# A four-layer graph kernel: VectorE takes the count tile of the next unit ahead of this unit's side items in the third layer, and one early maximum pass goes beside each unit

## Chip, cores and metric

One Trainium2 chip, one core of it. The metric is the time of one execution on the device in microseconds (us), as the median of several runs. A profile of one execution is read beside it.

## What is computed

A node table x of 3125 rows by 256 features goes through four layers, each of the form x = x + layer(max(layernorm(x), 0)), over one graph of 50000 edges (src, dst, weight):

```
L0: h + sum of neighbours -> (W1, batch norm, relu) -> (W2, batch norm, relu)
L1: two weighted graph convolutions with a root row, leaky relu, a linear layer
L2: x = norm * (h @ W.T + b);  out = norm * segment_sum(x[src], dst)
L3: a 4-head graph attention, graph norm, relu, a 1-head graph attention
```

`norm` is the degree to the power -1/2. The maximum in L3's softmax is taken over all neighbours of a node.

## The kernel before

**Blocks.** The nodes are 25 blocks (NB) of 125 (Q). After L0 the graph stands in DRAM as a dense matrix twice: `wt_d` (sums of weights) and `ct_d` (counts of edges as uint16, self loops included), each as 25 row blocks of 125 x 3125. The columns are taken in two halves of 13 and 12 blocks (HALF). A layer's aggregation is a dense product: a step k goes over one half of the columns, with 25 units, one for each row block j, and q = 25 k + j counts the units. L1 is the steps 0 to 3, and L2 the steps 4 (first half) and 5 (second half).

**A unit of L2.** SyncE loads a block of counts (L530). ScalarE casts it to float32 into one of three tiles TL (L1325); for unit q it waits until TensorE has done unit q-3, whose tile it was (L1324 and the lines around it). VectorE's `count_tile(q)` (from L1754) waits for the cast; if the block lies in this half it takes the self loops off its diagonal (L1764, which increments the semaphore `minus`), and it adds the tile, scaled by the norm, to a running sum cn (L1768, L1771). TensorE's `step_unit` waits for the cast, and, for a block in this half, for `minus`; then it multiplies (L984): 8 products in step 4, 6 in step 5, each of them two records in the trace. In step 4 the blocks j = 0 to 12 need `minus`, in step 5 the blocks 13 to 24.

**Side items.** Behind some units TensorE issues a side item (`aux_item`, L893 to L940), a small product that belongs to the step before or to what follows, and VectorE takes it in (`aux_in`). PLAN says behind which unit. Step 4 carries six output items of L1 behind units 2 to 7 (TensorE L937; VectorE L1712, L1715, L1717, and L1495 twice), behind unit 7 also the scales of the layer norm of the second half (`ln_scale`, L1504 to L1515; ScalarE then writes 12 blocks of H at L1218 ahead of its cast for unit 10), and the norms behind unit 10 (L893, L895). Step 5 carries seven output items of step 4 behind units 2 to 8 (L937, L940; VectorE L1725), then the transposes of L3's early scores behind units 11 to 17 (TensorE L904, VectorE L1674 or L1677) and the score products themselves behind units 13, 15, 17 and 18 (`early_scores`, L955, 52 records; VectorE `score_scales`, L1814 to L1819). Six more output items come after the last unit.

**Early maximum passes.** L3's maximum needs one pass of VectorE over every block of counts (`early_max`, L1827, and L1824 for the first of each half). The 26 passes of the first 13 blocks (EARLY) are taken early: EARLY_MAX puts one behind each odd unit and two behind each even one of j = 14 to 24 of step 5, 17 in all; one goes behind each of the six late output items, and the last three stand behind the scales of the last layer norm. Each has its counts from a DMA that GpSimd issues (L701) into one of three buffers, when the pass three before it is done. Behind them VectorE copies six banks of transposed features (L1879), which TensorE uses for the late scores (L1015), and then takes the late scales (L1814), on which the 24 late maximum passes wait, and through them L3's first unit.

**What sets the order.** Each engine runs its own instructions in the order in which they are written, and waits on semaphores. In the loop over q, VectorE's order was: `count_tile(q)`; the copies of the step before (`evac_f1`) at unit 2; the side items behind q; scales; maximum passes.

Of the kernel before, what the change touches and what calls it, by code (L numbers as in the profile page):

```python
# [17 lines left out]
NB = N // Q  # L18
# [53 lines left out]
LAYERS = 6  # L72
# [46 lines left out]
def gnn_stack(nc, x, src, dst, edge_weight, eps0, W01, b01, g01, be01, W02, b02, g02, be02,  # L119
              W11, b11, W12, b12, Wl1, bl1, root_idx, W2, b2, W31, as31, ad31, b31, gnw, gnb, gnms,  # L120
              W32, as32, ad32, b32, out):
    with ExitStack() as ctx:
        sems = {}

        def S(name):
            if name not in sems:
                sems[name] = ctx.enter_context(nc.semaphore(name))
            return sems[name]
# [164 lines left out]
        EARLY = [(j, half) for j in range(NE) for half in range(2)]  # L293
# [7 lines left out]
        EARLY_MAX = {}  # L301
        for j in range(14, NB):
            n0 = sum(len(v) for v in EARLY_MAX.values())
            EARLY_MAX[j] = range(n0, min(n0 + 1 + (j + 1) % 2, len(EARLY)))
        BESIDE = sum(len(v) for v in EARLY_MAX.values())


# [58 lines left out]
        for g_ in range(len(CB) + 1):  # L366
            if g_ < len(CB):
                HW_SEQ += [("turn", g_, k) for k in range(KT)]
            if g_:
                j, nj = CB[g_ - 1]  # L370
# [15 lines left out]
        def bank_of(f, c):  # L386
            return (f * 3 + c, 0) if c < 3 else (6, f * Q)
# [1017 lines left out]
        def _(dve):  # L1405
# [326 lines left out]
            def evac_f1(k):  # L1732

                dve.wait_ge(S("l12_pe"), (k + 1) * NB)
                if k:
                    dve.wait_ge(S("aux_pe"), LAST[k - 1] + 1)
                for c, (o, w) in enumerate(CHUNKS[k % 2][0:3]):
                    dst, src_ = aggL[:, 1, o:o + w], ps[:, bank_of(1, c)[0], 0:w]
                    if k // 2 == 1:
                        ts(dst, src_, colb[:, 1:2], None, ALU.add).then_inc(S("evD"), 1)  # L1740
                    else:
                        cp(dst, src_).then_inc(S("evD"), 1)
                if k // 2 != 1:
                    return
                for c, (o, w) in enumerate(CHUNKS[k % 2][0:3]):
                    t = aggL[:, 1, o:o + w]
                    dve.wait_ge(S("evD"), EVD[k] + c + 1)
                    stt(t, t, 0.01, t, ALU.mult, ALU.max).then_inc(S("f3D"), 1)
                for c, (o, w) in enumerate(CHUNKS[k % 2]):
                    t = aggL[:, 0, o:o + w] if c < 3 else aggL[:, :, o:o + w]  # L1750
                    dve.wait_ge(S("evA"), EVA[k] + c + 1)
                    stt(t, t, 0.01, t, ALU.mult, ALU.max).then_inc(S("f3A"), 1)

            def count_tile(q):  # L1754

                n = q - 4 * NB
                k, j = divmod(q, NB)
                h, w = k % 2, COLS[k % 2]
                j0, nj = HALF[h]
                dve.wait_ge(S("cast"), n + 1)  # L1760
                t = TL[q % TS][0:Q, 0:w]
                if j0 <= j < j0 + nj:
                    dg = t[:, (j - j0) * Q:(j - j0 + 1) * Q]
                    tt(dg, dg, ident[0:Q, 0:Q], ALU.subtract).then_inc(S("minus"), 1)  # L1764
                    dve.wait_ge(S("minus"), j + 1)
                c = cn[h][0:Q, 0:w]
                if j == 0:
                    ts(c, t, norm[0:Q, j:j + 1], None, ALU.mult).then_inc(S("cn_made"), 1)  # L1768
                else:
                    dve.wait_ge(S("cn_made"), n)  # L1770
                    stt(c, t, norm[0:Q, j:j + 1], c, ALU.mult, ALU.add).then_inc(S("cn_made"), 1)  # L1771

            def attention_columns():
                dve.wait_ge(S("w31_in"), 16)
                dve.wait_ge(S("att_in"), 32)
                for k in range(CT):
                    for w in range(2):
                        link(stt(att_junk, w32[:, k, 0:D], 1.0, att2[w], ALU.mult, ALU.mult,
                                 accum_out=w32[:, k, D + w:D + w + 1]))

                for k in range(KT):
                    for w in range(2):
                        for h in range(HEADS):
                            link(stt(att_junk, w31[:, k, h * D:(h + 1) * D], 1.0, att1[w][:, h * D:(h + 1) * D],
                                     ALU.mult, ALU.mult, accum_out=va[:, k, w * HEADS + h:w * HEADS + h + 1]))
                dve.sem_inc(S("va_made"), 1)
# [13 lines left out]
            def norm_factors():  # L1800

                dve.wait_ge(S("norms_sqrt"), 1)
                link(ts(kb[:, 1, 0:HEADS], kb[:, 1, 0:HEADS], 16.02, 1e-20, ALU.mult, ALU.add))
                link(ts(kb[:, 1, HEADS:HEADS + 1], kb[:, 0, HEADS:HEADS + 1], 1.001, 1e-20, ALU.mult, ALU.add))
                link(ts(kb[:, 2, :], kb[:, 1, :], 4.0, None, ALU.mult))
                link.mark(ts(kb[:, 3, :], kb[:, 1, :], -2.0 + 4e-6, None, ALU.mult))
                link(v_.reciprocal(kb[:, 0, :], kb[:, 2, :]))

            def score_scales(j0, nj, n):

                dve.wait_ge(S("ald_mm"), n)
                cols8 = ps[0:Q, 6, j0 * 2 * HEADS:(j0 + nj) * 2 * HEADS].rearrange("p (j w h) -> p w h j", w=2, h=HEADS)
                for h in range(HEADS):
                    link.mark(ts(asc[0:Q, 0, h * NB + j0:h * NB + j0 + nj], cols8[:, 0, h, :], kb[0:Q, 0, h:h + 1], 0.5,  # L1814
                                 ALU.mult, ALU.add))
                for row, by in ((1, 0.8), (2, 0.2)):
                    link.mark(ts(asc[0:Q, row, :].rearrange("p (h j) -> p h j", h=HEADS)[:, :, j0:j0 + nj], cols8[:, 0], by,
                                 None, ALU.mult))
                link(cp(ald[0:Q, j0:j0 + nj, :].rearrange("p j h -> p h j"), cols8[:, 1]))  # L1819

            def max_unit(t, dst, score, first, done, name):

                if first:
                    ts(dst, t, score, None, ALU.min).then_inc(S(name), 1)  # L1824
                else:
                    dve.wait_ge(S(name), done)
                    stt(dst, t, score, dst, ALU.min, ALU.max).then_inc(S(name), 1)  # L1827

            def early_max(r):

                j, half = EARLY[r]
                dve.wait_ge(S(f"hc_in{r % ES}"), 16 * (r // ES + 1))
                max_unit(EB[r % ES][0:Q, 0:COLS[half]], macc0[half][0:Q, :], asc[0:Q, 0, j:j + 1], j == 0, r - 1, "l3_max")

            for q in range(LAYERS * NB):
                k, j = divmod(q, NB)
                if q == 4:
                    attention_columns()
                    weight_norms()
                if q == 5 * NB + 7:  # L1840
                    norm_factors()
                if k >= 4:
                    count_tile(q)
                if k and j == (2 if k >= 4 else 0):
                    evac_f1(k - 1)
                for a in PLAN[k][j]:
                    aux_in(a)
                    if AUX[a][0] == "norms" or AUX[a][0][0] == "turn":
                        continue
                    if a == LAST[1]:  # L1850
                        link(v_.tensor_reduce(out=small[:, 28:30], in_=rootp[:, :, :], axis=AX_X, op=ALU.add))
                        dve.wait_ge(S("aux_pe"), 3)
                        root_row(small[:, 28:30], False)
                    if a == LAST[2]:
                        ln_scale(2, 0, True)
                    if a == LAST[3]:
                        ln_scale(2, 1, True)
                    if a == LAST[4]:
                        ln_scale(3, 0)
                if k == 5 and j in EARLY_S:  # L1860
                    score_scales(*CBE[EARLY_S[j]], EARLY_S[j] + 1)
                    dve.sem_inc(S("asc_made"), 1)
                if k == 5 and j in EARLY_MAX:
                    for r in EARLY_MAX[j]:
                        early_max(r)
            evac_f1(LAYERS - 1)
            left = BESIDE
# [4 lines left out]
                        early_max(left)  # L1872
                        left += 1
            ln_scale(3, 1)
            for r in range(left, len(EARLY)):
                early_max(r)
            for n, (k, j, nj) in enumerate(QG):
                dve.wait_ge(S("ring_pe"), base["h5"] + n + 1)
                cp(F[:, k, j * Q:(j + nj) * Q], ps[:, n % 4, 0:nj * Q]).then_inc(S("ring_ev"), 1)  # L1879
            score_scales(NE, NB - NE, len(CBE) + 1)  # L1880
            dve.sem_inc(S("asc_made"), 1)

# [260 lines left out]
```

## Time and profile before

| what | value |
|---|---|
| median of 3 runs | 3829.49 us (3829.3 to 3832.98) |
| the profiled execution, its own time | 3837.25 us |
| its span in the trace | 3835.4 us |
| TensorE, busy | 3410.9 us, 89% |
| VectorE, busy | 2364.9 us, 62% |
| ScalarE, busy | 840.5 us, 22% |
| GpSimd, busy | 665.3 us, 17% |
| step 4 of L2 | about 1522 to 1715 us of the span |
| step 5 of L2 | about 1717 to 1909 us |
| late output items, early and late passes up to L3's first unit | about 1909 to 2020 us |

PE is TensorE's matmuls, PEld its weight loads, DVE is VectorE, ACT ScalarE, POOL GpSimd, SP SyncE; a q behind the name is the engine's sequencer. Times of the trace are microseconds from the start of the span. A share of busy time is a mean over stages that have different limits, so each stage is to be read by itself.

### The profile page before, as it was taken

What the parts mean: (1) busy time and instruction counts of PE and PEld (TensorE: products, weight loads), DVE (VectorE), ACT (ScalarE), POOL (GpSimd) and SP (SyncE); (2) the same over time, 40 slices, a digit from 0 to 9 for tenths busy, and PEclk for the clock granted to TensorE, in tenths of its full rate; (3) what the DMA queues carried; (4) which work ended last, traced back from release to release, by engine and by line L of the source; (5) the groups of instructions that cost most, each with busy time, mean ns of one, the idle gap of its engine ahead of it and who ended that gap; (6) DMA issues with size and microseconds to landing.
All of it is one profiled execution on the core that took longest, in us unless ns stands there. A gap on an engine that the chain in (4) does not pass through costs nothing. (4 is left out here: it accounts for less than half of the span.)

```text
span 3835.4 us, 33927 instructions
## 1 busy us (share of the span) xinstructions
PE 3410.9 (89%) x12562; PEld 1933.5 (50%) x12562; DVE 2364.9 (62%) x3107; ACT 840.5 (22%) x1110; POOL 665.3 (17%) x489
## 2 busy tenths in 40 slices
PE   6999856887999999799739999999999999966998
PEld 6897644664554554445324444444444444454444
DVE  9973212245011121333589989988998898857997
ACT  0113312334000001222102222222222222242222
POOL 2788888840000000000000000000000000011000
PEclk9999978898999999899869999999999999987999
DMA  9999976994434344121352222222222232275222
GB/s 348 365 281 247 271 180 169 292 251 98 139 121 141 122 132 143 48 68 57 117 176 75 65 73 79 89 63 90 75 77 73 83 94 69 83 255 176 66 69 66
DMA packets 262143, 525.90 MB, mean 137 GB/s; under 512 B 91594, under 2 KB 152800, under 8 KB 260448
## 3 DMA queue, kind: packets, MB, share of 16 engines
q1 hardware_dynamic: 145817, 432.89, 34.9%
q0 software_dynamic: 63680, 30.84, 5.8%
q10 hardware_dynamic: 52480, 60.01, 5.7%
q8 instruction: 100, 1.64, 0.2%
q14 instruction: 66, 0.53, 0.0%
HBM read 361.99 MB, written 161.67 MB: 137 GB/s over the span
## 5 line engine op out<-in xcount | busy, mean ns | idle before, releaser
L1134 PE MATMUL ps<-R,B 125*128 125x500 f32 x2800 | 1099.2, 544 | 20.5 <-DVE R L2020 13.0
L1134 PEld LDWEIGHTS ps<-R,B 125*128 125x128 f32 x2800 | 505.6, 191 | 594.0 <-issue 546.9
L688 POOL DMA_INDIRECT pairs<-w x400 | 621.0, 1553 | 193.6 <-issue 105.8
L984 PE MATMUL ps<-R,H 125*128 125x500 f32 (+1 forms) x1400 | 575.6, 568 | 59.0 <-DVE R L1764 45.4
L1345 ACT ACTIVATE R<-R,asc 125x1625 f32<-125x1625 f32 (+1 forms) x200 | 320.2, 1601 | 1013.0 <-DVE R L2007 1013.0
L2020 DVE SCALAR_TENSOR_TENSOR R<-R 125x1625 f32<-125x1625 f32 (+1 forms) x250 | 445.1, 1780 | 0.0
L984 PEld LDWEIGHTS ps<-R,H 125*128 125x128 f32 x1400 | 265.9, 201 | 349.5 <-issue 346.8
L2007 DVE SCALAR_TENSOR_TENSOR R<-H,asc 125x1625 f32<-125x1625 f32 (+1 forms) x200 | 369.0, 1846 | 118.5 <-PE ps L1141 88.2
L837 PE MATMUL ps<-R,H 125*128 125x375 f32 (+1 forms) x1000 | 303.7, 451 | 99.0 <-DMA R<-pairs 98.6
L1134 PE MATMUL ps<-R,H 125*128 125x500 f32 (+1 forms) x700 | 274.6, 549 | 20.5 <-DVE R L2020 18.7
L706 POOL DMA_DIRECT2D B<-ct_d x50 | 27.1, 542 | 1525.0 <-PE ps L1134 1399.5
L1586 DVE TENSOR_TENSOR Fb<-Fb,ps 128x250 f32<-128x250 f32 (+1 forms) x140 | 67.2, 480 | 359.1 <-PE ps L837 290.3
L837 PEld LDWEIGHTS ps<-R,H 125*128 125x128 f32 x1000 | 186.8, 194 | 176.4 <-DMA R<-pairs 99.3
L984 PE MATMUL ps<-R,B 125*128 125x500 f32 (+1 forms) x700 | 266.8, 538 | 1.6 <-ACT R L1302 0.9
L1827 DVE SCALAR_TENSOR_TENSOR Fb<-R,asc,Fb 125x1625 f32<-125x1625 uint16 (+1 forms) x144 | 265.2, 1842 | 0.0
L1134 PEld LDWEIGHTS ps<-R,H 125*128 125x128 f32 x700 | 126.3, 193 | 162.6 <-issue 131.2
L984 PEld LDWEIGHTS ps<-R,B 125*128 125x128 f32 x700 | 126.9, 190 | 140.6 <-issue 139.4
L1476 DVE SCALAR_TENSOR_TENSOR R<-ps,Fb,R 125x500 bf16<-125x500 f32 (+3 forms) x400 | 191.0, 538 | 2.3 <-PE ps L781 2.3
L857 PE MATMUL ps<-ident,R 125*125 125x125 f32 x1250 | 170.4, 284 | 22.9 <-ACT B L1258 15.3
L701 POOL DMA_DIRECT2D Fb<-ct_d x9 | 5.1, 569 | 1040.1 <-PE ps L937 791.6
L857 PEld LDWEIGHTS ps<-ident,R 125*125 125x125 f32 x1250 | 160.7, 196 | 43.2 <-ACT B L1258 19.8
L1325 ACT ACTIVATE R<-R 125x1625 f32<-125x1625 uint16 (+1 forms) x50 | 75.0, 1505 | 331.1 <-PE ps L984 251.4
(309 smaller groups left out, 3093.9 us busy)
## 6 DMA issues: line engine op xcount, KB each, us to landing
pairs<-R SPq DMA_DIRECT2D x25, 3200.0 KB
R<-ct_d SPq DMA_DIRECT2D x162, 406.2 KB, 3.2
R<-pairs SPq DMA_DIRECT2D x25, 2500.0 KB
R<-ct_d SPq DMA_DIRECT2D x162, 375.0 KB, 3.1
R<-wt_d SPq DMA_DIRECT2D x50, 812.5 KB, 4.4
R<-wt_d SPq DMA_DIRECT2D x50, 750.0 KB, 4.2
wt_d<-R ACTq DMA_DIRECT2D x13, 1250.0 KB
wt_d<-B ACTq DMA_DIRECT2D x12, 1250.0 KB
```

The source lines that it names most:

```text
L688: pool.indirect_dma_start(pairs, bass.IndirectOffsetOnAxis(ap=key_u[:, c:c + 1], axis=0), val[:, c, :], None, compute_op=ALU.add)\
L837: last = mm(ps[:, n % 4, 0:w], H[0:Q, j0 + m, k * 128:(k + 1) * 128], pair_rows_at(i)[0:Q, m, o:o + w, 0], start=m == 0, stop=m == nb - 1 ...
L857: last = tr(ps[0:Q, 4 + 2 * (n % 2) + t, m * Q:(m + 1) * Q], pair_rows_at(i)[0:Q, m, b * Q:(b + 1) * Q, t], ident[0:Q, 0:Q])
L984: last = mm(ps[:, bank, at:at + w], rows[0:Q, j, f * 128:(f + 1) * 128], TL[q % TS][0:Q, o:o + w], start=j == 0 and at == 0, stop=j == NB ...
L1134: last = mm(ps[:, bank, at:at + w], rows[0:Q, j, f * 128:(f + 1) * 128], TT[q % TR][0:Q, o:o + w], start=j == 0 and at == 0, stop=j == NB ...
L1325: a(TL[q % TS][0:Q, 0:w], C16[n % CS][0:Q, 0:w], ACT.Copy).then_inc(S("cast"), 1)
L1345: a(t, t, ACT.Exp, bias=s2).then_inc(S("l3_exp"), 1)
L1476: stt(TW[c][:, b * CW + lo:(b + 1) * CW], ps[0:Q, (t % 2) * 2 + b, lo:CW], k, TRI[:, 0:CW - lo], ALU.is_equal, ALU.mult, accum_out=later[0 ...
L1586: tt(z, z, ps[:, n % 4, 0:w], ALU.add).then_inc(S("l0_ev"), 1)
L1827: stt(dst, t, score, dst, ALU.min, ALU.max).then_inc(S(name), 1)
L2007: stt(TT[q % TR][0:Q, 0:w], u[0:Q, 0:w], s8, u[0:Q, w:2 * w], ALU.add, ALU.max).then_inc(S("l3_a"), 1)
L2020: stt(t, t, 1.0, lc, ALU.min, ALU.mult).then_inc(S("l3_t"), 1)
```

## The change

In L2, VectorE takes `count_tile(q + 1)` in the iteration of unit q, ahead of the side items of q. The iteration of the last unit of step 3 takes the first tile, and the copies of the step before (`evac_f1`) now stand ahead of the tile. EARLY_MAX puts one maximum pass behind each of the units 14 to 24 of step 5, 11 in all. With one pass behind each of the six late output items there are then 9 left: four stand behind the scales of the last layer norm, as three did, and five behind the copies of the transposed features, ahead of the late scales. The other engines' programs are the same.

```diff
@@ -301,7 +301,7 @@
         EARLY_MAX = {}
         for j in range(14, NB):
             n0 = sum(len(v) for v in EARLY_MAX.values())
-            EARLY_MAX[j] = range(n0, min(n0 + 1 + (j + 1) % 2, len(EARLY)))
+            EARLY_MAX[j] = range(n0, n0 + 1)
@@ -1839,10 +1839,10 @@
                     norm_factors()
-                if k >= 4:
-                    count_tile(q)
                 if k and j == (2 if k >= 4 else 0):
                     evac_f1(k - 1)
+                if q + 1 >= 4 * NB and q + 1 < LAYERS * NB:
+                    count_tile(q + 1)
                 for a in PLAN[k][j]:
                     aux_in(a)
@@ -1872,11 +1872,13 @@
             ln_scale(3, 1)
-            for r in range(left, len(EARLY)):
+            for r in range(left, len(EARLY) - 5):
                 early_max(r)
             for n, (k, j, nj) in enumerate(QG):
                 dve.wait_ge(S("ring_pe"), base["h5"] + n + 1)
                 cp(F[:, k, j * Q:(j + nj) * Q], ps[:, n % 4, 0:nj * Q]).then_inc(S("ring_ev"), 1)
+            for r in range(len(EARLY) - 5, len(EARLY)):
+                early_max(r)
             score_scales(NE, NB - NE, len(CBE) + 1)
```

## Rows read from the trace of the kernel before

**Rows 1.** Waits, 1515 to 1965 us: total us, times, longest

```profile
PE ps L984 <- DVE R L1764: 45.4, 14, 5.2
```

**Rows 2.** Timeline, one period of step 4: start, duration, instruction, idle before and releaser

```profile
1582.44 0.69 DVE L1712 TENSOR_TENSOR PT<-ps,rootr 125x512 f32<-125x512 f32 x1 [8.60 <-PE ps L937]
...
1585.29 0.27 DVE L1764 TENSOR_TENSOR R<-R,ident 125x125 f32<-125x125 f32 x1
1585.60 1.91 DVE L1771 SCALAR_TENSOR_TENSOR Fb<-R,norm,Fb 125x1625 f32<-125x1625 f32 x1
...
1585.71 8.62 PE L984 MATMUL ps<-R,H 125*128 125x500 f32 x16 [3.30 <-DVE R L1764]
```

**Rows 3.** Timeline of L1, PE: an output item between two units

```profile
1264.68 5.64 PE L984 MATMUL ps<-R,B 125*128 125x500 f32 x16
1270.15 1.89 PE L937 MATMUL ps<-wA,Fb 128*125 128x256 f32 x8
1271.88 5.65 PE L984 MATMUL ps<-R,B 125*128 125x500 f32 x16
```

**Rows 4.** Timeline of step 4, PE: first and last output item, units 8 to 11

```profile
1540.75 1.89 PE L937 MATMUL ps<-wB,R 128*125 128x256 f32 x8
...
1607.82 1.89 PE L937 MATMUL ps<-wB,R 128*125 128x256 f32 x8
...
1614.91 18.66 PE L984 MATMUL ps<-R,H 125*128 125x500 f32 x48 [5.20 <-DVE R L1764]
1633.41 0.51 PE L893 MATMUL ps<-asb,ones 128*128 128x4 f32 x4
...
1636.25 78.60 PE L984 MATMUL ps<-R,H 125*128 125x500 f32 x224 [0.54 <-DVE R L1764]
```

**Rows 5.** Timeline of step 4, ACT: the cast for unit 10

```profile
1620.52 1.54 ACT L1325 ACTIVATE R<-R 125x1625 f32<-125x1625 uint16 x1
```

**Rows 6.** Timeline of step 5, PE: its start, units 12 to 14, units 19 to 24

```profile
1717.01 17.04 PE L984 MATMUL ps<-R,H 125*128 125x500 f32 x36 [2.16 <-ACT R L1304]
...
1797.09 0.59 PE L904 MATMUL ps<-ident,B 125*128 125x125 f32 x4
1797.51 5.20 PE L984 MATMUL ps<-R,H 125*128 125x500 f32 x12
1802.55 0.59 PE L904 MATMUL ps<-ident,B 125*128 125x125 f32 x4
1804.19 5.28 PE L984 MATMUL ps<-R,H 125*128 125x500 f32 x12 [1.06 <-DVE R L1764]
1809.31 1.81 PE L955 MATMUL ps<-va,wA 128*125 128x8 f32 x16
1810.97 0.62 PE L904 MATMUL ps<-ident,B 125*128 125x125 f32 x4
1813.67 6.86 PE L984 MATMUL ps<-R,H 125*128 125x500 f32 x12 [2.07 <-DVE R L1764]
...
1875.85 33.36 PE L984 MATMUL ps<-R,H 125*128 125x500 f32 x72 [5.00 <-DVE R L1764]
```

**Rows 7.** Windows, one unit of step 4: length, busy (x) by engine, granted clock

```profile
1558.39:1567.00 8.61, 8.61 (x17) 4.23 (x18) 1.80 (x1) 0.00 (x0) 0.00 (x0) 0.66 0.00 0
```

**Rows 8.** Timeline of L3, PE: narrow products and transposes between two units

```profile
2202.16 1.25 PE L1074 MATMUL ps<-ones,X 125*125 125x1 f32 x10
...
2203.58 5.20 PE L1134 MATMUL ps<-R,B 125*128 125x500 f32 x12
```

**Rows 9.** Timeline after L2, DVE: the last three early passes, copies, late scales

```profile
1940.30 1.78 DVE L1827 SCALAR_TENSOR_TENSOR wA<-R,asc,wA 125x1500 f32<-125x1500 uint16 x1
...
1945.52 3.60 DVE L1879 COPY Fb<-ps 128x500 f32<-128x500 f32 x6
1955.37 0.64 DVE L1814 TENSOR_SCALAR asc<-ps,kb 125x12 f32<-125x12 f32 x4 [6.25 <-PE ps L1015]
```

**Rows 10.** The line of GpSimd's loads of early counts, L701

```profile
DMA to landing us min/median/max: 3.1/3.5/4.7
```

## The prediction

> **What bounds the kernel now.** Of the page I took only where to look: TensorE works for most of the span, so the places where it stands still or runs slowly are what a change of order can win. The chain that ended last covers only about a quarter of the span, almost all of it in L3, so for L2 I went to the waits of that stage. There TensorE waits 14 times for L1764, the subtraction on the diagonal of a count tile, 45.4 us in all and up to 5.2 us at once [rows 1]. That is the first thing to see; what the wait is made of shows in the timeline. After a unit of step 4 TensorE issues the output item; VectorE takes it in from 1582.44 us in four kinds of operation, and only then gets to L1764 at 1585.29, though the tile had been cast long before; TensorE's next unit starts at 1585.71 after 3.30 us of standing still [rows 2]. So a unit is held by a side item that it doesn't need.
>
> The same pair of unit and output item without such a wait stands in L1: the unit takes 5.47 us (1264.68 to 1270.15), the item 1.73 (to 1271.88), together 7.20 [rows 3]. In step 4 the period is far longer than 7.20 + 3.30, because the unit itself takes 8.62 us [rows 2]: the windows give a granted clock of 0.66 for it, a mixture of the 1.2 and 2.4 GHz levels, after TensorE had stood still [rows 7]. The stall is thus paid twice.
>
> **Step 4.** The change puts L1764 and the sum of tile q+1 ahead of side item q. Its cast waits only for unit q-2, so it is there in time, and the item itself comes later than both. VectorE then has 2.85 us of item (1582.44 to 1585.29) and 2.2 us of tile (from there to the end of L1771) in 7.2 us [rows 2], so it does not become the bound. The first output item starts at 1540.75 and unit 3 can follow at 1542.48; five periods of 7.20 later unit 8 starts, at 1578.48, where it started at 1614.91 [rows 4]: **36.4 us** won. What is late next is the H that units 13 on read, and through it the cast for unit 10, which ScalarE has queued behind it. It depends on the last item: that began on TensorE at 1607.82 [rows 4], 1.73 ahead of the place where unit 8 can now start, T, and the cast ended at 1622.06 [rows 5], so at T + 12.5; with the subtraction unit 10 can start at T + 12.85. Units 8 and 9 are through at T + 10.94. A stall of 1.9 us appears that the late start of unit 8 had hidden.
>
> Does such a gap cost clock? Gaps of 1.06 us were followed by a unit at full pace (5.28 us), gaps of 2.07 and 2.16 were not: 6.86 us for a unit of 5.04, which is 1.8 lost, and 17.04 for three units of 15.12 [rows 6]. 1.9 is nearest to these, so I charge 1.8. Units 8 to 10 then take 3 x 5.47 + 1.9 + 1.8 = 20.1 us in place of 18.50 (1614.91 to 1633.41), a loss of 1.6; the wait of 0.54 ahead of unit 11 goes [rows 4]. Unit 11 keeps its slow start, since the norms' narrow products ahead of it stay. Step 4 in sum: 36.4 - 1.6 + 0.5 = **35.3 us**. The bounds of the doubtful part are 0 and 3.0 for the clock around this stall.
>
> **Step 5.** Units 3 to 8 don't need the subtraction and have no such wait; nothing is won. From unit 13 on each unit again stood behind a side item, the scales and one or two maximum passes. TensorE was free for unit 13 at 1804.19 - 1.06 = 1803.13, and unit 24 ended at 1875.85 + 33.36 = 1909.21 [rows 6]. Without waits and at full clock: 12 units of 5.04 (1797.51 to 1802.55) are 60.5; three blocks of early scores of 1.66 (1809.31 to 1810.97) and a fourth with a quarter of the products, 5.4; four turns of 0.42 and a half one, 1.9 [rows 6]. The sum is 67.8, so the end is at 1870.9, **38.3 us** earlier. Can VectorE keep up? Beside a unit without scores it has a tile of 2.2 us [rows 2] and one pass of 1.74 (three from 1940.30 to 1945.52 [rows 9]), which leaves 1.1 of 5.04 for the copy of a turn. The tightest place is a unit with scores: unit 13 ended at 1809.31, and with the turn and the scales taken in and no pass the subtraction let unit 14 start at 1813.67, 4.4 later [rows 6]; a pass makes it 6.1. TensorE has scores, turn, the next unit and its turn until then, 2.08 + 5.04 + 0.42 = 7.5 us. With two passes it would be 7.8 and too late. So the order and the single pass are both needed here, and together leave no wait.
>
> The clock is open again: a block of scores with its turn is 2.08 us of narrow products (8 columns) and transposes. A stretch of 1.42 us of that kind in L3 (2202.16 to 2203.58) left the next unit at 5.20 us [rows 8]; standing still for 2.16 us did not [rows 6]. 2.08 lies close to the upper one in length, but TensorE works in it, so I charge half of 1.8 for each of three blocks, 2.7, with the bounds 0 and 5.4. Step 5: 38.3 - 2.7 = **35.6 us**.
>
> **After L2.** The six late output items carry one pass each as before; nothing changes. But six passes fewer have been made. One more than before stands ahead of the copies, on a path where VectorE is busy without a break; it is one over the wider half, and I take +1.8. Five stand behind the copies, at 1.74 each 8.7 us, where VectorE had stood idle for 6.25 us until the late scores came [rows 9]; the overhang is 2.5. The late scores, 1.8 later themselves, come before the five passes are through and stay hidden. And the passes now come in runs of four and five, with three buffers: a load starts when the pass three before it has ended, and two passes, 3.5 us, are then all that covers 3.5 us to landing (median) [rows 10] and GpSimd's issue before it. I take a wait of 0.5 in each run, 1.0 in all, between 0 and 2.5. The give-back is 1.8 + 2.5 + 1.0 = **5.3 us**, between 4.3 and 6.8. The 24 late passes and all of L3 follow as they were.
>
> For such a load the Trainium skill (DMA: Bandwidth & Descriptors, the fixed and variable parts of a DMA's time) gives about 2.0 us and the bytes at 436 GB/s, by which the 416 KB of 128 x 1625 counts of two bytes would take 3.0 us, an estimate. By it the runs would hardly wait and the give-back would be 4.3 us; the row shows 3.5 us, and the sum above goes by the row.
>
> **The sum.** 35.3 + 35.6 - 5.3 = 65.6 us less. The durations are those of the profiled execution, 3837.25 us by its own time with a span of 3835.4; it stands 7.8 above the median of the runs, 3829.49. The same saving taken from the median gives **3764 us**.
>
> **Rivals.**
> *The wait moves on.* TensorE could wait for the cast, or VectorE for it with a side item queued behind, so that only about half is won. For it: the new stall at unit 10 is of this kind. Against it: the waits name no cast ahead of units 3 to 8 of step 5, where only the cast gates a unit, and a cast may start two units ahead. Half of 70.9 less 5.3 is 30 us saved: 3799 us. Chance 0.05.
> *The clock doesn't come back.* The stalls go but the units behind the items stay at the lower level for some 3 us each, as behind a stall. Against it speaks L1, where the same item is followed by a unit at full pace [rows 3]. Price: five times 8.62 - 5.47 in step 4 [rows 2, 3], 15.8 us, and in step 5 five units at 1.8 where 2.7 us are charged already, 6.3 us; together 22, so 3786 us. Chance 0.04.
> *Slower.* The place is the run of passes behind L2. If both steps were held by something else than the place of the count tile, they would win nothing, while six passes of about 1.8 us have been taken out of time that was hidden beside TensorE and put ahead of L3: +5.3 us for what can be hidden, 3835 us. It decides from the point where L2 wins less than 5.3 us. Rows 1 name L1764 as what TensorE waited for, 45.4 us, so this needs the trace to be misread. Chance 0.02.
> *The change doesn't do what it says:* VectorE could stand before `count_tile(q + 1)` because the cast isn't ready, and so be no earlier. At unit 10 it does so; elsewhere the cast lies one unit or more back. This would be the first or the third case, and has no more chance than they.
>
> **How the numbers follow.** The forecast has 0.89. Its own bounds: the best is no clock lost at unit 10 and behind the scores and no waits for loads, 65.6 + 1.8 + 2.7 + 1.0 = 71, or 3758; the worst is 65.6 - 1.2 - 2.7 - 1.5 = 60, or 3769. Two microseconds of scatter of the runs at the lower end, and above it room for a stall that I haven't seen, give 3756 to 3777. The rivals lie outside, with some 0.1. A difference under 0.2%, 7.7 us, is about what a measurement of this kernel can't tell from none. Faster by more 0.96, the same 0.02, slower 0.02.
>
> **What would show it.** In the changed kernel's trace TensorE's wait for L1764 falls from 45 us to a few, all at unit 10; starts of units 3 to 8 are 7.2 us apart with a granted clock of 1.00; unit 13 to the end of unit 24 takes 68 to 73 us; VectorE's idle time ahead of the late scales is gone and the last pass ends about 5 us later relative to the end of L2. The prediction is wrong if the starts of units 3 to 8 stay over 10 us apart, if TensorE waits for the cast instead, or if VectorE waits for more than 3 us for the early counts.

## The result, and the profile after

| | before | changed |
|---|---|---|
| median | 3829.39 us (4 runs, 3827.49 to 3832.98) | 3768.11 us (4 runs, 3762.41 to 3769.75) |
| the profiled execution, its own time | 3837.25 us | 3762.41 us |
| its span | 3835.4 us | 3760.5 us |
| TensorE, busy | 3410.9 us | 3374.7 us |

The ratio is 0.9836, with a 95% interval from 0.982 to 0.9852: 61 us less in the medians, 65.6 forecast. The measured median lies inside the predicted range, 4 us above the forecast.

The waits of the changed kernel from 1515 to 1965 us (total us, times, longest), those on the count tile and on the counts' loads:

```profile
DVE wA L1827 <- DMA R<-ct_d: 4.9, 1, 4.9
...
DVE PT L1827 <- DMA wB<-ct_d: 2.0, 1, 2.0
...
PE ps L984 <- DVE R L1764: 1.8, 1, 1.8
```

TensorE's wait for the subtraction has gone from 45.4 us in 14 pieces [rows 1] to one of 1.8. Waits of VectorE for the counts of its early passes are new. The timeline of TensorE in step 4 (start, duration, instruction, idle before and releaser), which answers to [rows 4]:

```profile
1537.42 1.89 PE L937 MATMUL ps<-wB,R 128*125 128x256 f32 x8
1539.15 5.65 PE L984 MATMUL ps<-R,H 125*128 125x500 f32 x16
1544.64 1.89 PE L937 MATMUL ps<-wB,R 128*125 128x256 f32 x8
1546.37 5.64 PE L984 MATMUL ps<-R,H 125*128 125x500 f32 x16
...
1575.21 11.14 PE L984 MATMUL ps<-R,H 125*128 125x500 f32 x32
1588.19 5.71 PE L984 MATMUL ps<-R,H 125*128 125x500 f32 x16 [1.84 <-DVE R L1764]
1593.73 0.51 PE L893 MATMUL ps<-asb,ones 128*128 128x4 f32 x4
...
1595.89 77.07 PE L984 MATMUL ps<-R,H 125*128 125x500 f32 x224
```

The units start 7.2 us apart and take 5.65 us, where one took 8.62 [rows 2]. The one gap is at unit 10, and unit 10 runs at full pace behind it (granted clock 1.00 from 1588.19 to 1593.90). Step 5 from unit 13 on, against [rows 6]:

```profile
1675.11 15.34 PE L984 MATMUL ps<-R,H 125*128 125x500 f32 x36 [2.16 <-ACT R L1304]
...
1759.38 5.21 PE L984 MATMUL ps<-R,H 125*128 125x500 f32 x12
1764.42 1.81 PE L955 MATMUL ps<-va,wA 128*125 128x8 f32 x16
1766.09 0.63 PE L904 MATMUL ps<-ident,B 125*128 125x125 f32 x4
1766.55 5.21 PE L984 MATMUL ps<-R,H 125*128 125x500 f32 x12
...
1797.01 30.46 PE L984 MATMUL ps<-R,H 125*128 125x500 f32 x72
```

From the start of unit 13 to the end of unit 24 it is 68.1 us (1759.38 to 1827.47), without a gap. Behind L2, VectorE's timeline answers to [rows 9]:

```profile
1864.17 1.91 DVE L1827 SCALAR_TENSOR_TENSOR PT<-R,asc,PT 125x1625 f32<-125x1625 uint16 x1 [0.21 <-DMA R<-ct_d]
1866.00 3.60 DVE L1879 COPY Fb<-ps 128x500 f32<-128x500 f32 x6
1869.51 1.77 DVE L1827 SCALAR_TENSOR_TENSOR wA<-Fb,asc,wA 125x1500 f32<-125x1500 uint16 x1
1873.33 1.91 DVE L1827 SCALAR_TENSOR_TENSOR PT<-wB,asc,PT 125x1625 f32<-125x1625 uint16 x1 [2.04 <-DMA wB<-ct_d]
1880.15 1.78 DVE L1827 SCALAR_TENSOR_TENSOR wA<-R,asc,wA 125x1500 f32<-125x1500 uint16 x1 [4.91 <-DMA R<-ct_d]
...
1885.36 0.64 DVE L1814 TENSOR_SCALAR asc<-ps,kb 125x12 f32<-125x12 f32 x4
```

The late scales start 57.9 us after the end of unit 24; before it was 46.2 (1909.21 to 1955.37). That is 11.7 us given back, where 5.3 was forecast. What the loads met shows in the view of the DMA from 1860 to 1886 us (out and in, issuing engine, count, KB each, us from issue to landing) and in SyncE's timeline:

```profile
x_d<-X SPq DMA_DIRECT2D x1, 2800.0 KB
R<-ct_d POOLq DMA_DIRECT2D x1, 406.2 KB, 3.4
wB<-ct_d POOLq DMA_DIRECT2D x1, 406.2 KB, 9.0
Fb<-ct_d POOLq DMA_DIRECT2D x1, 406.2 KB, 9.7
Fb<-ct_d POOLq DMA_DIRECT2D x1, 375.0 KB, 3.5
R<-ct_d POOLq DMA_DIRECT2D x1, 375.0 KB, 13.8
```

```profile
1864.83 0.82 SPq L569 DMA_DIRECT2D x_d<-X  x2
```

At 1864.83 us SyncE begins to store X, and loads that took 3.5 us take 9.0 to 13.8. The store starts as soon as the last layer norm is written (ScalarE's L1218 ends at 1864.80). In the kernel before it began at the same place, at 1946.46, but the last early load had been issued at 1939.13, and none came behind it.

In sum, from the first unit of step 4 to the first of L3 (1522.54 to 2022.58 before, 1520.89 to 1952.58 after) it is 500.0 against 431.7 us: 68.3 us less. The two profiled executions differ by 74.8: 1.7 came before that stretch and 4.9 behind it, in L3, whose program is unchanged. I take this for scatter: the profiled execution is the shortest of the four. Over the profiled executions of all ten kernels the start of step 4, up to which TensorE's program is the same, lies between 1516.0 and 1526.6 us.

### The profile page after: what moved, and what is told of

Its sections match the earlier page's. It is cut to its first block and busy times, and to the rows that moved or that the text cites. A ratio compares the mean times of both kernels' runs of the same rounds, so it can differ in the third digit from the quotient of the medians.

```text
span 3760.5 us, 33927 instructions
## 1 busy us (share of the span) xinstructions
PE 3374.7 (90%) x12562; PEld 1921.5 (51%) x12562; DVE 2365.2 (63%) x3107; ACT 839.9 (22%) x1110; POOL 664.5 (18%) x489
## 5 line engine op out<-in xcount | busy, mean ns | idle before, releaser
L984 PE MATMUL ps<-R,H 125*128 125x500 f32 (+1 forms) x1400 | 542.8, 542 | 15.1 <-ACT H L1218 7.6
L984 PEld LDWEIGHTS ps<-R,H 125*128 125x128 f32 x1400 | 253.3, 191 | 283.7 <-issue 280.7
L1134 PE MATMUL ps<-R,H 125*128 125x500 f32 (+1 forms) x700 | 276.1, 551 | 20.0 <-DVE R L2022 18.3
L837 PEld LDWEIGHTS ps<-R,H 125*128 125x128 f32 x1000 | 186.6, 194 | 173.3 <-DMA R<-pairs 96.3
L1134 PEld LDWEIGHTS ps<-R,H 125*128 125x128 f32 x700 | 127.0, 194 | 163.0 <-issue 132.1
L701 POOL DMA_DIRECT2D Fb<-ct_d x9 | 4.9, 545 | 979.5 <-PE ps L937 756.5
L792 PE MATMUL ps<-Fb,R 125*125 125x4 bf16 x1000 | 128.3, 248 | 18.6 <-DVE R L1476 17.1
```

Source lines behind the costliest of these rows:

```text
L792: last = mm(ps[0:Q, 4 + t % 2, c * 4:(c + 1) * 4], TW[c0][:, c * Q:(c + 1) * Q], vals[:, t * SC + c0, :], start=c0 == 0 and c == 0, stop=c ...
L837: last = mm(ps[:, n % 4, 0:w], H[0:Q, j0 + m, k * 128:(k + 1) * 128], pair_rows_at(i)[0:Q, m, o:o + w, 0], start=m == 0, stop=m == nb - 1 ...
L984: last = mm(ps[:, bank, at:at + w], rows[0:Q, j, f * 128:(f + 1) * 128], TL[q % TS][0:Q, o:o + w], start=j == 0 and at == 0, stop=j == NB ...
L1134: last = mm(ps[:, bank, at:at + w], rows[0:Q, j, f * 128:(f + 1) * 128], TT[q % TR][0:Q, o:o + w], start=j == 0 and at == 0, stop=j == NB ...
```

## Experiments

**Order alone (e1).** The kernel before with only this edit; 17 passes beside step 5 and the tail are as before:

```diff
-                if k >= 4:
-                    count_tile(q)
                 if k and j == (2 if k >= 4 else 0):
                     evac_f1(k - 1)
+                if q + 1 >= 4 * NB and q + 1 < LAYERS * NB:
+                    count_tile(q + 1)
```

> The kernel before with only the count tile taken one unit ahead; 17 passes beside step 5 and three behind L2, as before. My theory now: the two passes stand behind even units, which carry no scores except unit 18, and there fit (0.6 + 0.7 + 3.6 us, then the subtraction at about 5.2 us, due at 5.5), so step 5 from unit 13 takes 68 to 70 us and nothing is given back behind L2: 46 us from the end of L2 to the late scales. Total 11 us under the changed kernel, about 3757. The rival, which the prediction stated: with two passes VectorE is late, TensorE waits for L1764 in most even units of step 5 and loses clock; step 5 from unit 13 takes 75 us or more and the total is 3763 or more.

Measured: 3756.26 us (5 runs), ratio 0.9805 (0.9791 to 0.9819), 76 us less. TensorE in step 5 and VectorE at its end and behind it:

```profile
1766.76 5.21 PE L984 MATMUL ps<-R,H 125*128 125x500 f32 x12
...
1804.39 30.56 PE L984 MATMUL ps<-R,H 125*128 125x500 f32 x72
```

```profile
1833.24 1.91 DVE L1827 SCALAR_TENSOR_TENSOR PT<-wB,asc,PT 125x1625 f32<-125x1625 uint16 x1
1835.06 1.84 DVE L1742 COPY R<-ps 128x500 f32<-128x500 f32 x3
...
1880.35 0.64 DVE L1814 TENSOR_SCALAR asc<-ps,kb 125x12 f32<-125x12 f32 x4 [6.98 <-PE ps L1015]
```

Step 5 from unit 13 takes 68.2 us (1766.76 to 1834.95) with 17 passes beside it, as with 11, and the late scales come 45.4 us after its end. The order gives the whole gain of L2; the second half of the change only costs. VectorE's last pass ends within 0.2 us of TensorE's last unit: in the changed kernel VectorE had stood idle there for 6.8 us.

**Passes alone (e2).** The changed kernel with `count_tile(q)` at its old place (the edit of e1, reversed).

> The changed kernel with the old order of the count tile: 11 passes beside step 5 and nine behind L2. Steps 4 and 5 keep their stalls. If order is what wins, step 4 is as in the kernel before (92.7 us from the first output item to the norms); in step 5 each even unit waits 1.8 us less and some clock comes back, some 9 to 15 us won, and 11.7 us are given back behind L2: 3825 to 3832 us, no difference that can be told. The rival, that one pass a unit brings a good part of the gain by itself, would give under 3815.

Measured: 3834.59 us (11 runs), ratio 1.001 (1.0001 to 1.0019). The waits of its stretch 1515 to 1960 us:

```profile
PE ps L984 <- DVE R L1764: 40.1, 14, 5.2
```

The stalls stay. Units 13 to 24 take 98.6 us in place of 105.0, from the timeline: 6.4 us won, less than the 9 to 15 that I expected. The late scales come 57.7 us after their end: 11.5 us given back. The time is 0.1% longer. That is within the 0.2% that the prediction calls no difference, but the interval lies just above 1, and the median above the 3825 to 3832 us expected.

**The store later (e3).** The changed kernel with

```diff
+            sp.wait_ge(S("l3_max"), len(EARLY) - 1)
             for p0, p1 in PART:
                 sp.dma_start(x_d[p0:p1, :], Xf[p0:p1, :]).then_inc(S("x_out"), 16)
```

> The changed kernel with SyncE's store of X to DRAM (3.2 MB) begun only when 25 of the 26 early passes are done. If the store is what held the loads of the last early counts, VectorE's waits of 2.04 and 4.91 us for them fall under 0.7 each, and the late scales start some 6 us earlier after the end of L2 (52 us in place of 57.9), with up to 2 us lost again where late counts queue behind the store: 3762 to 3764 us. The rival, that GpSimd's issue and three buffers are too slow for five passes in a run by themselves, leaves waits of 5 us or more and the time at 3768.

Measured: 3758.32 us (5 runs), ratio 0.9813 (0.98 to 0.9827). The five passes and the late scales (lines are one higher, and waits stand in brackets):

```profile
1868.88 1.77 DVE L1828 SCALAR_TENSOR_TENSOR wA<-Fb,asc,wA 125x1500 f32<-125x1500 uint16 x1
1870.57 1.91 DVE L1828 SCALAR_TENSOR_TENSOR PT<-wB,asc,PT 125x1625 f32<-125x1625 uint16 x1
1872.39 1.77 DVE L1828 SCALAR_TENSOR_TENSOR wA<-R,asc,wA 125x1500 f32<-125x1500 uint16 x1
1874.42 1.91 DVE L1828 SCALAR_TENSOR_TENSOR PT<-Fb,asc,PT 125x1625 f32<-125x1625 uint16 x1 [0.26 <-DMA Fb<-ct_d]
1876.52 1.78 DVE L1828 SCALAR_TENSOR_TENSOR wA<-wB,asc,wA 125x1500 f32<-125x1500 uint16 x1 [0.19 <-DMA wB<-ct_d]
1878.22 0.64 DVE L1815 TENSOR_SCALAR asc<-ps,kb 125x12 f32<-125x12 f32 x4
```

The waits of 2.04 and 4.91 are down to 0.3 and less, and the late scales start 51.2 us after the end of step 5 (1796.56 + 30.46 to 1878.22). So the store was the cause, and GpSimd with three buffers is fast enough. Without the collision 5.0 us are given back, against the 5.3 of the prediction. The median fell by some 10 us, more than the 6.7 us of this stretch and below the 3762 to 3764 expected; the two profiled executions differ by 7.2. What the rest of the 10 is I can't say from these runs.

**All nine passes ahead of the copies (e4).** The changed kernel with its two loops of the left passes made one, ahead of the copies.

> The changed kernel with all nine left passes ahead of the copies of the transposed features. The loads are then through before the store is far along, but the late scores wait for the copies: nine passes are 15.7 us and two or three waits of 0.2 to 0.5 us, copies 3.6 us and scores about 6 to 10 us behind them: late scales 56 to 60 us after the end of L2, no better than the changed kernel's 57.9, 3766 to 3771 us. If the store delays nothing, the changed kernel's placing would be the better by 6 us: 3774.

Measured: 3777.42 us (4 runs), ratio 0.9861 (0.9842 to 0.9879): slower than the changed kernel (all four times lie above its four, though the intervals of the ratios overlap), and worse than expected. Two of the passes and the scales:

```profile
1873.90 1.91 DVE L1827 SCALAR_TENSOR_TENSOR PT<-wB,asc,PT 125x1625 f32<-125x1625 uint16 x1 [5.25 <-DMA wB<-ct_d]
...
1881.57 1.78 DVE L1827 SCALAR_TENSOR_TENSOR wA<-R,asc,wA 125x1500 f32<-125x1500 uint16 x1 [5.76 <-DMA R<-ct_d]
...
1899.42 0.64 DVE L1814 TENSOR_SCALAR asc<-ps,kb 125x12 f32<-125x12 f32 x4 [9.04 <-PE ps L1015]
```

My expectation overlooked that the store waits for ScalarE's layer norm and not for the copies: it begins at 1865.45 us and runs into these loads as well, and now the copies and the scores stand behind the two waits. The late scales come 71.2 us after the end of step 5. Given nine passes, the place that the change chose for five of them is the better one.

**Two passes behind every unit (e8).** Order alone with

```diff
-            EARLY_MAX[j] = range(n0, min(n0 + 1 + (j + 1) % 2, len(EARLY)))
+            EARLY_MAX[j] = range(n0, n0 + 2)
```

> Order alone with two passes behind every unit from 14 on in step 5, 22 in all, and four behind the late output items. By the prediction two passes do not fit behind a unit with scores: the subtraction comes 7.8 us after the end of units 15 and 17, due at 7.5, and units 19 to 24 need 5.5 us of VectorE each against 5.04: TensorE waits for L1764 some 0.3 to 0.6 us a unit, step 5 from unit 13 takes 71 to 73 us in place of 68, and the time is 3758 to 3762. If VectorE's tiles taken ahead still cover it, step 5 stays at 68 to 69 and the time at that of e1.

Measured: 3754.74 us (4 runs), ratio 0.9806 (0.9791 to 0.9821). Its waits from 1515 to 1960 us, TensorE's units 17, 19, 20 and 24, and VectorE behind the last of them:

```profile
PE ps L984 <- DVE R L1764: 4.8, 8, 1.8
```

```profile
1781.73 5.28 PE L984 MATMUL ps<-R,H 125*128 125x500 f32 x12 [0.18 <-DVE R L1764]
...
1794.78 5.28 PE L984 MATMUL ps<-R,H 125*128 125x500 f32 x12 [0.48 <-DVE R L1764]
1801.32 5.28 PE L984 MATMUL ps<-R,H 125*128 125x500 f32 x12 [1.27 <-DVE R L1764]
...
1823.44 5.27 PE L984 MATMUL ps<-R,H 125*128 125x500 f32 x12 [0.25 <-DVE R L1764]
```

```profile
1832.15 1.84 DVE L1742 COPY R<-ps 128x500 f32<-128x500 f32 x3
...
1876.65 0.64 DVE L1814 TENSOR_SCALAR asc<-ps,kb 125x12 f32<-125x12 f32 x4 [6.40 <-PE ps L1015]
```

Here VectorE becomes the bound: units 20 to 24 start 5.53 us apart in place of 5.04, and seven waits of 0.2 to 1.3 us stand in front of units 17 and 19 to 24. None costs clock. From unit 13 on step 5 takes 72.6 us (1756.11 to 1828.71), as expected, against 68.2 with order alone. The two passes behind unit 24 then hold the copies at the end of step 5 until 1832.15, and the late scales come 47.9 us after its end, against 45.4. So in this trace it is 7.0 us more from unit 13 to the late scales than with order alone. The medians don't show it: 3754.74 us is below the expected 3758 to 3762 and beside the 3756.26 of order alone. The own times of the two profiled executions (3752.87 and 3760.11 us) hide it as well, because that of order alone came to step 4 later, by 10.6 us. Whether 22 passes cost anything against 17 is therefore open: the trace says 7 us, the times say nothing. That 11 cost something, both say.

**Scores twice (e5).** The changed kernel with each block of early scores computed twice, into the same place:

```diff
-                for j in range(j0, j0 + nj):
+                for j in 2 * list(range(j0, j0 + nj)):
```

> The changed kernel with each block of early scores computed twice into the same place, so that the stretch of narrow products ahead of units 14, 16 and 18 is 3.3 us and a turn in place of 1.7 us and a turn. In the changed kernel these units ran at full pace (5.2 us). If narrow products count as standing still for the clock, which the half charge of 2.7 us in the prediction assumed in part, 3.7 us of them must do what a stall of 3.3 us did: the next unit takes 6.9 us or more and its window shows a granted clock under 0.8. If they count as work, it stays at 5.2 us. The products themselves add 5.4 us to step 5 either way.

One execution, 3765.85 us. TensorE's timeline around units 14, 16 and 18 (a turn is the transposes, L904):

```profile
1761.08 3.56 PE L955 MATMUL ps<-va,wA 128*125 128x8 f32 x32
...
1764.96 6.90 PE L984 MATMUL ps<-R,H 125*128 125x500 f32 x12
...
1777.15 3.56 PE L955 MATMUL ps<-va,wA 128*125 128x8 f32 x32
...
1781.03 5.21 PE L984 MATMUL ps<-R,H 125*128 125x500 f32 x12
...
1795.20 6.90 PE L984 MATMUL ps<-R,H 125*128 125x500 f32 x12
```

Units 14 and 18 take 6.90 us, each with a granted clock of 0.75; unit 16, behind the same work, takes 5.21 at 1.00. So 3.4 us of products of 8 columns and a turn lowered the clock in two cases of three. The 1.66 us of the changed kernel did not: in the seven profiles where such a block and its turn stand alone ahead of a unit, all 21 units take 5.2 us. Step 5 from unit 13 takes 77.2 us in place of 68.1: 5.7 for the products and 3.4 for the clock. The expectation allowed for the first; the time of the one execution doesn't show either.

**The normalised blocks one cast later (e6).** Order alone with one constant changed, the cast of L2 behind which ScalarE writes them:

```diff
-        LNAT = 9
+        LNAT = 10
```

> Order alone (e1) and ScalarE writes the normalised blocks after its cast for unit 10 in step 4 (11 in step 5), one cast later. If the stall of 1.84 us at unit 10 and the one of 0.74 us at unit 11 of step 5 are due to those casts queued behind the normalised blocks, both go and nothing takes their place: 2.6 us under e1, about 3753.5. The rival: the normalised blocks, which the transposes and the units from 13 on wait for, come later and a wait of like size appears there: the time of e1, 3756.

Measured: 3750.95 us (5 runs), ratio 0.9794 (0.978 to 0.9807). Two stalls were its aim: the 1.84 us at unit 10 of step 4, and one of 0.74 to 0.76 us for a cast (L1325) at unit 11 of step 5, which the kernel before has too. In the window from 1560 to 1600 us (length, busy of TensorE first, granted clock after the engines) TensorE has no gap, and units 9 to 11 of step 5 are one block:

```profile
1560.00:1600.00 40.00, 40.00 (x141) 22.93 (x140) 25.19 (x40) 15.36 (x19) 1.73 (x3) 1.00 0.30 94
```

```profile
1738.64 15.27 PE L984 MATMUL ps<-R,H 125*128 125x500 f32 x36
```

Both stalls are gone and none took their place. The medians are 5 us apart, though the intervals of e1 and e6 overlap, so the 2.6 us are shown by the trace and not by the times.

**Three passes moved from ahead of the copies (e7).** e6 with two of them behind `evac_f1` at the end of step 5 and one behind the copies of the features:

```diff
             left = BESIDE
+            for r in range(left, left + 2):
+                early_max(r)
+            left += 2
...
             ln_scale(3, 1)
-            for r in range(left, len(EARLY)):
-                early_max(r)
...
+            for r in range(left, len(EARLY)):
+                early_max(r)
             score_scales(NE, NB - NE, len(CBE) + 1)
```

> e6 with the three passes that stood ahead of the copies of the transposed features moved: two behind the copies at the end of step 5, where VectorE waits 4.8 us for the first output item, and one behind the copies of the features. VectorE has 5.2 us less ahead of the copies. If it sets when the late scores start, they come up to 2 us earlier; if ScalarE's normalised blocks do, whose last group the transposes waited 0.33 us for in e1, 0.5 us or less. I expect the second: 3753 us, no difference to e6.

Measured: 3748.95 us (5 runs), ratio 0.9795 (0.9781 to 0.9809). The late scales come 45.4 us after the end of step 5 (1826.03 to 1871.47), in e6 44.9: taking 5.2 us of VectorE's work away from there wins nothing. The scores wait for the normalised blocks and for TensorE's own narrow products. e6 and e7 are the best versions found: their medians are 17 and 19 us under the changed kernel, and from the start of step 4 to the first unit of L3 they take 12.5 and 12.0 us less than its 431.7. What the rest of the difference is these traces don't show.

## Why the prediction was right, and where its steps were off

**Step 4: right to a microsecond, but for the clock.** Foreseen were periods of 7.20, the new stall of 1.9 at unit 10 and a net gain of 35.3. Measured from the first output item to unit 11: 95.5 us before (1540.75 to 1636.25), 58.5 after (1537.42 to 1595.89), 37.0 less. The stall is 1.84. The failed term is "1.9 is nearest to these, so I charge 1.8": unit 10 took 5.71 us in the changed kernel and in the five experiments that have this gap too. One of the two gaps that the charge was read from, the one of 2.07, also stood behind 2.08 us of narrow products. "Unit 11 keeps its slow start" was wrong as well: the block from unit 11 on took 78.6 us before and in e2, and 77.1 in the changed kernel and in all seven other experiments, in which the wait of 0.54 us ahead of it is gone. The mechanism of the stall at unit 10 is shown by e6.

**Step 5: right, the clock term again not paid.** 67.8 us of work forecast, 68.1 measured, 36.9 less than before and 1.06 more for the wait of unit 13. "I charge half of 1.8 for each of three blocks, 2.7" measured 0; e5 shows that the doubt was justified and only the length was too short.

**"The order and the single pass are both needed here": false.** e1 has two passes behind each even unit and loses nothing. The tight place was reckoned for a unit with scores, and "with two passes it would be 7.8 and too late" is about right there: e8, with two passes behind units 15 and 17, has waits of 0.18 and 0.48 us at units 17 and 19, and neither costs clock. But the old plan put only one pass behind units 15 and 17 and none behind 13. Behind an even unit VectorE has no scales to take ahead of its passes (unit 18 has a short block). The prediction costed a case that the kernel doesn't have and so took the second half of the change for a necessary part. Against the kernel before, e1 and the changed kernel differ by 0.9805 to 0.9836: about 12 us that the change gives away.

**After L2: the term for loads was too small.** "I take a wait of 0.5 in each run, 1.0 in all, between 0 and 2.5" measured 7.2 us (0.21, 2.04, 4.91), beyond its own bounds. The give-back of 11.7 us lies outside its "between 4.3 and 6.8" too, and one of the prediction's own signs of being wrong came true: VectorE waited for more than 3 us for the early counts. So the forecast of the time holds, and the account of this stretch doesn't. It asked how long a load takes, and not what else is on the DMA then. That the store of X begins right there stood in the code and in the trace of before. With the store out of the way (e3) the waits are 0.8 in all and the give-back 5.0.

**What evened out.** In the stretch as a whole 68.3 us were won where 65.6 were forecast. Clock not lost at unit 10 and behind the scores (+4.5), clock kept at unit 11 (+1.5), and clock kept by the luck of this execution at the start of steps 4 and 5 (+1.7 and +1.7, see below) outweighed the 6.2 us that the loads cost in excess. The median, 61 us less, lies nearer to the forecast than the terms deserve, and that is luck too.

**The rivals.** A new wait for a cast came at unit 10 and nowhere else. The clock came back behind every item. For the slower case L2 would have had to win less than is given back; e2 is that case, with the order taken away: 6.4 us won and 11.5 given back, and its median lies 2.4 us above the 3832.24 of the kernel before.

## What to carry to other kernels

When an engine waits for a small result that another one makes late in its queue, move that result ahead of work nobody waits for, and count separately what each further edit in the same change brings: here the move alone was worth 76 us, and the rebalancing that came with it took 12 back. Before hidden work is moved out to a quieter place, ask which transfers start there: a bulk store that nobody had waited for made loads of 0.4 MB take 2.6 to 3.9 times as long (9.0 to 13.8 us against 3.5).

## What was unexpected of the hardware

**The same gap does not always cost clock.** TensorE's wait of 2.36 us at the start of step 4 is in the profiles of all ten kernels; the three units behind it took 18.4 us in seven of them (granted clock 0.91 in the kernel before) and 16.7 in three (1.00 in the changed kernel). Behind the wait of 2.16 us at the start of step 5 it was 17.0 us five times and 15.3 five times. After 1.84 us the clock stayed in all six. After 2.03 us behind a turn, and 2.07 us behind scores and a turn, a unit of 5.2 us took 6.9 in all three cases (the kernel before and e2). After the 3.3 us ahead of each of the units 3 to 7 it fell nine times in ten (again in the kernel before and in e2). So in these traces waits between about 2 and 3.3 us cost clock in some executions and not in others, with the same work around them, and this alone shifts an execution of this kernel by some 3 us.

**Narrow products can cost clock too.** 3.4 us of them and a turn lowered the clock twice and spared it once (e5). At unit 11 of step 4 the norms' products, 2.16 us, left the granted clock at 1.00 in the changed kernel; in the kernel before 2.30 us of them and a wait of 0.54 stood ahead of the same unit, and it was 0.73 for the next 5.8 us, as in e2. The longer stall at unit 8 has gone in the changed kernel as well, so that the 0.54 us alone are to blame is likely and not shown.
